# Last row of the third filter tap by TensorE, w1T loaded in three pieces, last blocks of P shared anew

## The chip, the cores and the metric

The kernel runs on one core of a Trainium2 chip. The time is that of the device in microseconds; the kernel before takes 394.8 us (median of three runs, 394.65 to 394.81).

## The reference, cut to what matters

The input x has 16 images of 32 x 32 pixels and 128 channels, in float32. A depthwise 3x3 convolution gives three values a channel (w_perc), a matrix w_up1 takes these 384 to 256 hidden values, then comes an exact GELU, w_up2 back to 128, and the sum with x is h. On h lies a 3x3 windowed attention with w_qkv, and its result is added.

```python
perceived = conv(x, w_perc, groups=C, padding='SAME') + b_perc      # 3C channels
hid = gelu(einsum('bphw,dp->bdhw', perceived, w_up1) + b_up1)       # 2C
h = x + einsum('bdhw,cd->bchw', hid, w_up2) + b_up2
qkv = h @ w_qkv.T + b_qkv
scores = [ (q * shifted(k, dy, dx)).sum(-1) / sqrt(C) for 9 places ]
out = h + sum(softmax(scores)[i] * shifted(v, dy, dx))
```

The depthwise filter and w_up1 are both linear, so the kernel joins them into one 3x3 convolution from 128 to 256 channels.

## The kernel before, in words

**Weights.** For each horizontal tap i (0, 1, 2) and row dy (0, 1, 2) the joined weight is the sum over m of wg[:, m, dy, i] times w1T[:, m, :], where w1T holds w_up1 (128 partitions, three groups m of 256) and wg the filters times -1/6 (L946). Tap 0 and tap 2 are built by ScalarE (m = 0, first_products, L746) and VectorE (m = 1 and 2, L1012), row by row; tap 1 by TensorE (middle_tap, L451) out of nine diagonal matrices that ScalarE makes from the identity (L767). VectorE and ScalarE combine the three taps into six sets of Winograd weights (weff, L1021 to L1041), each split into a high part (whi, L775) and a low part (wlo, L993, L999), as products are taken in fp32r three times over (high x high, high x low, low x high).

**Images.** An image lies as four planes of columns (xp). VectorE forms ab (L960, L962) and four parts of t (transform, L970), GpSimd differences of planes (fc, ge, L1381 to L1385) and two more parts of t (L1389, L1390). ScalarE rounds t to thi (L715), VectorE (GpSimd for image 0) forms tlo (L977). TensorE's products (L484) go in units: an image has two halves of the hidden channels with six units each, and a unit has nine products of up to 256 columns. The sums are taken back by VectorE: combine (ps_sb and ru_sb, L1057, L1058), combine_y (L1067 to L1073) and finish_y (L1081). Then ScalarE's GELU (L731), its rounding (high_hid, L741), the low part on GpSimd (low_hid, L1404), the products up (L539), the sum h (sum_h, L1238), its high and low parts (L816, L987), q, v and scores on TensorE (L575 to L592), the maxima (L1111) and exponentials (L807), the normalising of p on GpSimd (L1411), and its transposition into ptc (turn_p, L1145). Blocks of ptc are moved into pt by DMA (L414, 12 an image); for the last two images these moves are copies, by ScalarE (place, L796), VectorE (L1160) and GpSimd (L1474). The products with v (values, L609) come two images later.

**Order.** It is written by hand for every engine, on each a list of its own in body(n, ...), with images 0 to 3 apart, a loop of ten images, and the last two apart; `last` holds what follows. An engine's instructions start in this order, and semaphores tie the engines together. All large loads are issued by SyncE's queue in program order, w1T first, x_planes of image 0 next; the filters (L708) and the identity (L709) go over ScalarE's queue. All stores are issued by SyncE, the last seven in store_late (L399, L404).

**TensorE's start.** It waits for w1T, issues five fillers (keep_busy, ten passes, as a float32 product takes two), the middle tap (18 passes), small products for the biases and for wq.wk, three more fillers into m_ps (L471, after which VectorE may write there), and then the first products of image 0.

Of the kernel before, what the change touches and what calls it, by code (L numbers as in the profile page):

```python
# [14 lines left out]
P = 128  # L15
# [68 lines left out]
def build(nc, x_planes, x_rows, w_perc, b_perc, w1_c, b_up1, w2_c, b_up2, wqk_c, wv_c, b_qkv, ident_bf_c,  # L84
          mask_c, zero_c, out):
    with ExitStack() as ctx:
# [104 lines left out]
        diag = y_flat[:, 0:9 * P].rearrange("p (m d c) -> p m d c", m=3, d=3)  # L191
        end0 = by_row(ptc[:, :, :].rearrange("p t k -> p (t k)"))
# [5 lines left out]
        first_in = sem("first_in")  # L198
# [16 lines left out]
        tap1_done = sem("tap1_done")  # L215
        first_done = sem("first_done")
# [47 lines left out]
        hlo_done = sem("hlo_done")  # L264
        h_hi_done = sem("h_hi_done")
# [94 lines left out]
        def _(sp):  # L360
# [10 lines left out]
            sp.dma_start(w1T[:, :, :].rearrange("p m d -> p (m d)"), w1_c).then_inc(first_in, 16)  # L371
# [23 lines left out]
            def store_late():  # L395

                for i, (n, g) in enumerate(LATE):
                    sp.wait_ge(o_done, (B - 3) * 2 + i + 1)
                    sp.dma_start(out[n][:, g * CH:(g + 1) * CH],  # L399
                                 o_of(n)[:, g * CH:(g + 1) * CH]).then_inc(stored[g], 16)  # L400
# [35 lines left out]
        def _(pe):  # L436
# [7 lines left out]
            def middle_tap():  # L444

                pe.wait_ge(first_in, 16)
                keep_busy(5)
                for dy in range(3):
                    pe.wait_ge(diag_done, 3 * dy + 3)
                    for m in range(3):  # L450
                        last = pe.matmul(acc[1][:, dy, :], diag[:, m, dy, :], w1T[:, m, :], start=(m == 0),  # L451
                                         stop=(m == 2))
# [82 lines left out]
            def up(n):  # L535
# [20 lines left out]
                pe.wait_ge(hlo_done, n * 2)  # L556
# [57 lines left out]
            def last_attention():  # L614
# [40 lines left out]
                for g in range(2):  # L655
                    pe.wait_ge(pt_done, 12 + 6 * g)
                    pe.wait_ge(pt_dve_done, 12 + 3 * g)
                    if g:
                        pe.wait_ge(pt_pool_done, 3)
# [47 lines left out]
        def _(act):  # L707
# [15 lines left out]
            def gelu(n, half):  # L723
# [4 lines left out]
                if from_image(n, 1):  # L728
# [14 lines left out]
            def first_products(i):  # L743

                for dy in range(3):
# [14 lines left out]
            act.wait_ge(first_in, 16)  # L760
            act.wait_ge(filters_done, 1)
            for i in TAPS:
                first_products(i)
            act.wait_ge(ident_in, 16)
            for dy in range(3):
# [72 lines left out]
            def last():  # L838
# [10 lines left out]
                for g in range(2):  # L849
# [4 lines left out]
                    for row in (0, 1):  # L854
                        place(1, row, range(4 * g, 4 * g + 4))

# [86 lines left out]
        def _(dve):  # L943
# [4 lines left out]
            dve.wait_ge(first_in, 16)  # L948
# [40 lines left out]

            def low_weights(j, k):  # L990
# [12 lines left out]
            for k, i in enumerate(TAPS):  # L1003

                for m in (1, 2):
                    for dy in range(3):
                        if m == 1:
                            dve.wait_ge(first_done, dy + 1 if k == 0 else 6)
# [11 lines left out]
            dve.wait_ge(acc_done, 12)  # L1020
# [152 lines left out]
            def last():  # L1173
# [22 lines left out]
                sums(n, 1)  # L1196
# [320 lines left out]
```

## Time and profile before

| | |
|---|---|
| median of 3 runs | 394.8 us |
| profiled execution | 394.93 us |
| its span | 393.1 us |
| TensorE busy | 382.4 us, 97% |
| TensorE's weight loads | 359.6 us, 91% |
| VectorE busy | 340.3 us, 87% |
| ScalarE busy | 256.5 us, 65% |
| GpSimd busy | 180.0 us, 46% |

The time is that of the whole execution, the span runs from the first instruction to the last. Busy shares are averages over the span and over stages that differ: read them by stretches.

### The profile page before, as it was taken

Reading aid. Unit: us, or ns where it says so; the run is one execution under the profiler, and the core shown is the slowest. Engines: PE = TensorE matmul, PEld = TensorE weight load, DVE = VectorE, ACT = ScalarE, POOL = GpSimd, SP = SyncE. Lnnn points to the kernel's source line nnn. Section 1 sums busy time; section 2 is a strip of 40 time slices with the busy share of each in tenths; the row PEclk is TensorE's granted clock in tenths of the full one; section 3 lists DMA queues with packets and bytes.
Section 4 is the critical chain, followed back from the end, with each engine's and each line's share of the span. In section 5 each row is a group of like instructions: output and inputs, shape, how many; then the busy total and the mean of one; then the engine's idle time right before and its main releaser. Section 6 shows DMA issues by size and latency. Waiting matters only on the chain.

```text
span 393.1 us, 10470 instructions
## 1 busy us (share of the span) xinstructions
PE 382.4 (97%) x3664; PEld 359.6 (91%) x3664; DVE 340.3 (87%) x919; ACT 256.5 (65%) x542; POOL 180.0 (46%) x159
## 2 busy tenths in 40 slices
PE   5999999999999999999999999999999999999995
PEld 4999998999989999999999999999999999999874
DVE  4999999999988889888888988888898888887795
ACT  6645478929485774848477484847748484773893
POOL 5784563646445262635525263552526355132111
PEclk9999999999999999999999999999999999999999
DMA  7420301434151513325150332515033231403003
GB/s 226 183 67 3 121 2 25 139 45 170 31 187 20 171 32 65 141 39 173 25 181 14 74 131 39 173 26 175 21 71 132 39 107 26 121 12 85 3 27 135
DMA packets 56313, 33.98 MB, mean 86 GB/s; under 512 B 47200, under 2 KB 48096, under 8 KB 56288
## 3 DMA queue, kind: packets, MB, share of 16 engines
q1 hardware_dynamic: 56000, 33.61, 30.3%
q8 instruction: 15, 0.25, 0.3%
q10 hardware_dynamic: 288, 0.05, 0.1%
q14 instruction: 10, 0.08, 0.1%
HBM read 19.86 MB, written 8.39 MB: 72 GB/s over the span
## 4 chain that ended last, share of the span: by engine, by line
PE 83%; DVE 11%; issue 2%; DMA 1%; ACT 1%; POOL 0%; DVEq 0%; ACTq 0%
PE m_ps L484 45%; PE work L539 10%; PE s_ps L609 9%; PE work L583 7%; PE s_ps L592 6%; PE s_ps L578 2%; PE s_ps L575 2%; PE s_ps L576 2%; DVE t L970 1%; DMA wp<-w_perc 1%; DVE tlo L977 1%; DVE h_around L1238 1%; DVE h_lo L987 1%; DVE s_ps L1012 1%; PE work L562 1%
## 5 line engine op out<-in xcount | busy, mean ns | idle before, releaser
L484 PE MATMUL m_ps<-thi,whi 128*128 128x256 f32 x558 | 158.9, 285 | 0.9 <-DVE ru_sb L1058 0.8
L484 PE MATMUL m_ps<-thi,wlo 128*128 128x256 f32 x558 | 155.5, 279 | 0.0
L484 PE MATMUL m_ps<-tlo,whi 128*128 128x256 f32 x558 | 154.3, 276 | 0.0
L484 PEld LDWEIGHTS m_ps<-thi,whi 128*128 128x128 f32 x558 | 104.8, 188 | 4.3 <-issue 1.0
L484 PEld LDWEIGHTS m_ps<-tlo,whi 128*128 128x128 f32 x558 | 105.6, 189 | 0.6
L484 PEld LDWEIGHTS m_ps<-thi,wlo 128*128 128x128 f32 x558 | 104.9, 188 | 0.0
L1404 POOL TENSOR_TENSOR hid_lo<-hid,hid_hi 128x1024 fp32r<-128x1024 f32 x30 | 72.2, 2406 | 27.9 <-ACT hid_hi L741 21.4
L1381 POOL TENSOR_TENSOR fc<-xp 128x512 f32<-128x512 f32 x16 | 21.3, 1333 | 98.3 <-DVE tlo L977 91.8
L731 ACT ACTIVATE hid<-y,b1eff 128x1024 f32<-128x1024 f32 x31 | 35.7, 1152 | 33.1 <-DVE y L1081 23.1
L715 ACT CAST thi<-t 128x1024 fp32r<-128x1024 f32 (+1 forms) x32 | 25.1, 832 | 48.6 <-DVE t L970 48.5
L807 ACT ACTIVATE p_sb<-p_sb,negmax 128x101 f32<-128x101 f32 x128 | 46.8, 369 | 6.2 <-DVE negmax L1111 6.1
L1411 POOL TENSOR_TENSOR p_sb<-p_sb,rsum 128x384 f32<-128x384 f32 x32 | 27.8, 870 | 42.7 <-DVE rsum L1134 42.7
L609 PE MATMUL s_ps<-pt,v_sb 128*128 128x192 f32 (+2 forms) x260 | 39.0, 305 | 0.0
L609 PEld LDWEIGHTS s_ps<-pt,v_sb 128*128 128x128 f32 x260 | 37.3, 190 | 0.0
L1057 DVE TENSOR_TENSOR ps_sb<-m,m_ps 128x512 f32<-128x512 f32 x32 | 21.6, 676 | 13.9 <-ACT m L721 13.9
L816 ACT CAST h_hi<-h_around 128x512 fp32r<-128x512 f32 x30 | 18.3, 621 | 22.3 <-DVE h_around L1238 22.2
L741 ACT CAST hid_hi<-hid 128x1024 fp32r<-128x1024 f32 x30 | 31.5, 1050 | 0.2
L583 PEld LDWEIGHTS work<-wvT,h_around 128*128 128x128 f32 x240 | 29.1, 192 | 1.2
L977 DVE TENSOR_TENSOR tlo<-t,thi 128x1024 fp32r<-128x1024 f32 (+1 forms) x30 | 28.7, 999 | 1.3 <-ACT thi L715 1.3
L583 PE MATMUL work<-wvT,h_around 128*128 128x129 f32 x240 | 29.2, 275 | 0.0
L1089 DVE TENSOR_TENSOR v_sb<-work,bv 128x384 f32<-128x384 f32 (+1 forms) x45 | 23.0, 512 | 6.3 <-PE work L583 5.2
L823 ACT ACTIVATE q_sb<-s_ps,bq_s 128x512 f32<-128x512 f32 x30 | 20.6, 688 | 11.4 <-PE s_ps L578 11.3
(156 smaller groups left out, 765.6 us busy)
## 6 DMA issues: line engine op xcount, KB each, us to landing
xp<-x_planes SPq DMA_DIRECT2D x16, 640.0 KB, 5.3
xr<-x_rows SPq DMA_DIRECT2D x16, 512.0 KB, 4.1
out<-o_sb SPq DMA_DIRECT2D x28, 256.0 KB, 4.0
pt<-ptc SPq DMA_DIRECT2D x140, 32.0 KB, 1.9
pt<-ptc SPq DMA_DIRECT2D x28, 28.0 KB, 1.9
out<-y SPq DMA_DIRECT2D x3, 256.0 KB, 2.5
w1T<-w SPq DMA_DIRECT2D x1, 384.0 KB, 3.6
out<-y SPq DMA_DIRECT2D x2, 128.0 KB, 2.4
```

What stands on the lines that cost most here:

```text
L484: last = pe.matmul(bank[:, col + first:col + end], a[:, j, dy, half * P:(half + 1) * P], c[:, par, T_PLACE[j], first + by:end + by], start ...
L539: return pe.matmul(up_bank(n, c), w[:, half * C:(half + 1) * C], h[:, half, c * CH:(c + 1) * CH], **kw)
L583: last = pe.matmul(v_bank(n, part)[:, u * VT:(u + 1) * VT], h_of(n - 1, hp)[:, W + i * P:W + (i + 1) * P], wvT[:, :], start=True, stop=True)
L592: last = pe.matmul(s[row * W:(row + 1) * W, u, :], q_sb[:, q:q + W], h_of(n - 1, hp)[:, q:q + NEAR], start=True, stop=True, skip_group_che ...
L609: last = pe.matmul(o_bank(n, g)[:, (first - g * half) * W:(end - g * half) * W], v_of(n - 3, hp)[:, i, :], pt[:, hp, i, (first - above) * ...
L715: nc.scalar.copy(thi[:, par, part, :], t[:, part, :]).then_inc(thi_done, 1)
L731: nc.scalar.activation(hid[:, half, :].rearrange("p (r k s) -> p k r s", k=K4, s=WIN), y[:, half, :, :].rearrange("p k (r s) -> p k r s", ...
L741: nc.scalar.copy(hid_hi[:, half, :], hid[:, half, :]).then_inc(hhi_done, 1)
L807: nc.scalar.activation(p_sb[:, i, 0:KEYS], p_sb[:, i, 0:KEYS], ACT.Exp, bias=negmax[:, i:i + 1], scale=-1.0, accum_out=p_sum[:, i:i + 1]). ...
L977: nc.vector.tensor_tensor(tlo[:, par, part, :], t[:, part, :], thi[:, par, part, :].bitcast(F32), ALU.subtract).then_inc(tlo_done, 1)
L1404: nc.gpsimd.tensor_tensor(hid_lo[:, half, :], hid[:, half, :], hid_hi[:, half, :].bitcast(F32), ALU.subtract).then_inc(hlo_done, 1)
L1411: nc.gpsimd.tensor_tensor(p_sb[:, tiles, 0:NEAR], p_sb[:, tiles, 0:NEAR], rsum[:, tiles].unsqueeze(2).to_broadcast([P, 4, NEAR]), ALU.mult ...
```

## The change

In words: w1T comes by three DMAs, each with a semaphore of its own. ScalarE makes three diagonals (row_diag) for the last row (dy = 2) of tap 2, and TensorE forms this row out of them ahead of the middle tap; ScalarE and VectorE no longer do. The fillers before it are three instead of five, and the middle tap waits for each diagonal instead of for three. In image 0 GpSimd's differences for image 2 wait until the first four parts of y are done. The low part of the second half of hid of image 0 is formed by VectorE (low_hid_first). In image 2 combine(2, 1) stands between the two groups of maxima. Behind the last image the turn of P's second half comes before VectorE's blocks; GpSimd takes row 3 of tiles 0 to 3 instead of 4 to 7, VectorE row 2 of tiles 0 to 3 and rows 2 and 3 of tiles 4 to 7. The stores of image 14 are issued by ScalarE's queue.

```diff
-            sp.dma_start(w1T[:, :, :].rearrange("p m d -> p (m d)"), w1_c).then_inc(first_in, 16)
+            for m in range(3):
+                sp.dma_start(w1T[:, m, :], w1_c[:, m * HID:(m + 1) * HID]).then_inc(w1_in[m], 16)
...
                 for i, (n, g) in enumerate(LATE):
+                    if n == B - 2:
+                        continue
...
-                pe.wait_ge(first_in, 16)
-                keep_busy(5)
+                pe.wait_ge(w1_in[0], 16)
+                keep_busy(3)
+                for m in (1, 2):
+                    pe.wait_ge(w1_in[m], 16)
+                for m in range(3):
+                    pe.wait_ge(row_diag_done, m + 1)
+                    last = pe.matmul(acc[2][:, 2, :], row_diag[:, m, :], w1T[:, m, :], start=(m == 0), stop=(m == 2))
+                last.then_inc(tap2_done, 1)
                 for dy in range(3):
-                    pe.wait_ge(diag_done, 3 * dy + 3)
                     for m in range(3):
+                        pe.wait_ge(diag_done, 3 * dy + m + 1)
...
-                pe.wait_ge(hlo_done, n * 2)
+                if is_image(n, 1):
+                    pe.wait_ge(hlo_dve_done, 1)
+                else:
+                    pe.wait_ge(hlo_done, n * 2)
...
-                    pe.wait_ge(pt_dve_done, 12 + 3 * g)
-                    if g:
-                        pe.wait_ge(pt_pool_done, 3)
+                    pe.wait_ge(pt_dve_done, 9 + 6 * g)
+                    pe.wait_ge(pt_pool_done, 3)
...
-            for i in TAPS:
-                first_products(i)
+            first_products(0)
             act.wait_ge(ident_in, 16)
+            for m in range(3):
+                nc.scalar.activation(row_diag[:, m, :], ident_bf[:, :], ACT.Copy,
+                                     scale=wg[:, m, 2, 2:3]).then_inc(row_diag_done, 1)
+            first_products(2, range(2))
...
+                act.wait_ge(o_done, (B - 1) * 2)
+                for g in range(2):
+                    act.dma_start(out[B - 2][:, g * CH:(g + 1) * CH],
+                                  o_of(B - 2)[:, g * CH:(g + 1) * CH]).then_inc(stored[g], 16)
...
+            def low_hid_first():
+                dve.wait_ge(hhi_done, 2)
+                nc.vector.tensor_tensor(hid_lo[:, 1, :], hid[:, 1, :], hid_hi[:, 1, :].bitcast(F32),
+                                        ALU.subtract).then_inc(hlo_dve_done, 1)
...
-                    for dy in range(3):
+                    dve.wait_ge(w1_in[m], 16)
+                    for dy in range(3 - k):
                         if m == 1:
-                            dve.wait_ge(first_done, dy + 1 if k == 0 else 6)
+                            dve.wait_ge(first_done, dy + 1 if k == 0 else 5)
...
+            dve.wait_ge(tap2_done, 1)
             nc.vector.tensor_tensor(sum02, tap0, acc[2], ALU.add).then_inc(sums_done, 1)
...
                 sums(n, 1)
+                add_h(n, 1, 1)
+                turn_p(n, 1)
                 dve.wait_ge(ptc_done, n * 2 - 1)
                 dve.wait_ge(o_ready, n * 2 - 4)
+                place(1, 2, range(0, 4))
+                dve.wait_ge(ptc_done, n * 2)
                 for row in (2, 3):
-                    place(1, row, range(0, 4))
-                turn_p(n, 1)
-                add_h(n, 1, 1)
-                dve.wait_ge(ptc_done, n * 2)
-                place(1, 2, range(4, 8))
+                    place(1, row, range(4, 8))
...
-                for g in range(2):
-                    add_zero_keys(n, g)
-                    row_max(n, 1 - par, g, g + 1)
+                add_zero_keys(n, 0)
+                row_max(n, 1 - par, 0, 1)
+                if is_image(n, 2):
+                    combine(2, 1)
+                add_zero_keys(n, 1)
+                row_max(n, 1 - par, 1, 2)
...
                     combine_y(1, 0)
+                    low_hid_first()
                     transform_ab(2, 0)
...
                     sums_ab(1)
+                    pool.wait_ge(y_part_done, 4)
                     differences(2, 0)
                     pool.wait_ge(y_part_done, 8)
                     low_hid(0, 0)
                     return
                 if is_image(n, 1):
-                    low_hid(0, 1)
...
-                pool.wait_ge(ptc_done, B * 2)
+                pool.wait_ge(pn_done, B * 2)
+                pool.wait_ge(ptc_done, B * 2 - 1)
                 pool.wait_ge(o_ready, B * 2 - 4)
-                for rows, there, cols, to_rows, to_there, to_cols in p_blocks(3, range(4, 8)):
+                for rows, there, cols, to_rows, to_there, to_cols in p_blocks(3, range(0, 4)):
```

## Rows read from the trace of the kernel before

**Rows 1.** Busy time by stages: stretch, busy us of TensorE, granted clock, DMA, GB/s

```profile
90.00:360.00 270.00, 269.67 (x2673) 1.00 0.32 88
```

**Rows 2.** Chain of waits, first 40 us: start us, us, what

```profile
0.74 3.77 DMA wp<-w_perc
...
10.11 0.79 DVE s_ps L1012 x2
...
13.87 0.96 DVE m_ps L1024
```

**Rows 3.** TensorE's loads by line: ns min/median/max, first to last start

```profile
L442 PEld LDWEIGHTS work<-w1T x10: 285/337/337, 4.4 to 7.8; 128*128 128x128 f32 x10
...
L451 PEld LDWEIGHTS work<-w1T,y x18: 190/190/337, 8.3 to 12.9; 128*128 128x128 f32 x18
```

**Rows 4.** Timeline of TensorE's loads: start us, us, instruction, idle before

```profile
16.78 0.19 PEld L484 LDWEIGHTS m_ps<-thi,whi 128*128 128x128 f32 x1 [0.17 <-issue]
```

**Rows 5.** DMA issues, first 16 us: queue, KB each, median us to landing

```profile
xp<-x_planes SPq DMA_DIRECT2D x3, 640.0 KB, 4.9
...
w1T<-w SPq DMA_DIRECT2D x1, 384.0 KB, 3.6
...
ident_bf<-identity_bf ACTq DMA_DIRECT2D x1, 32.0 KB, 5.1
zeros<-zero_keys SPq DMA_DIRECT2D x1, 20.0 KB, 2.1
wp<-w_perc ACTq DMA_DIRECT2D x1, 13.5 KB, 3.8
```

**Rows 6.** Timeline of ScalarE, 4 to 10 us

```profile
4.82 1.27 ACT L746 ACTIVATE m_ps<-w1T,wg 128x256 f32<-128x256 f32 x3 [1.64 <-DVE wg L946]
...
7.23 2.72 ACT L767 ACTIVATE y<-ident_bf,wg 128x128 f32<-128x128 bf16 x9
```

**Rows 7.** Timeline of TensorE's loads, after the first products: idle in brackets

```profile
29.54 0.19 PEld L484 LDWEIGHTS m_ps<-thi,whi 128*128 128x128 f32 x1 [0.21 <-issue]
...
34.39 0.19 PEld L484 LDWEIGHTS m_ps<-thi,whi 128*128 128x128 f32 x1 [0.62 <-issue]
...
73.79 0.19 PEld L484 LDWEIGHTS m_ps<-thi,whi 128*128 128x128 f32 x1 [0.58 <-DVE ru_sb L1058]
```

**Rows 8.** Timeline of VectorE and GpSimd, 28 to 75 us

```profile
28.01 2.56 DVE L977 TENSOR_TENSOR tlo<-t,thi 128x1024 fp32r<-128x1024 f32 x2
...
38.65 2.64 DVE L1071 SCALAR_TENSOR_TENSOR y<-ru_sb 128x256 f32<-128x256 f32 x1
...
67.43 1.81 DVE L977 TENSOR_TENSOR tlo<-t,thi 128x1024 fp32r<-128x1024 f32 x2
...
72.46 0.68 DVE L1057 TENSOR_TENSOR ps_sb<-m,m_ps 128x512 f32<-128x512 f32 x1
...
38.61 2.41 POOL L1404 TENSOR_TENSOR hid_lo<-hid,hid_hi 128x1024 fp32r<-128x1024 f32 x1 [0.50 <-ACT hid_hi L741]
...
72.01 2.38 POOL L1404 TENSOR_TENSOR hid_lo<-hid,hid_hi 128x1024 fp32r<-128x1024 f32 x1
```

**Rows 9.** Timelines behind the last image, by engine

```profile
382.82 2.00 DVE L1160 COPY pt<-ptc 32x128 f32<-32x128 f32 x6
384.85 0.58 DVE L1145 STREAM_TRANSPOSE ptc<-p_sb 128x384 f32<-128x384 f32 x1
...
386.81 1.23 DVE L1214 TENSOR_TENSOR y<-m_ps,h_around 128x1024 f32<-128x1024 f32 x1
...
382.87 0.85 POOL L1411 TENSOR_TENSOR p_sb<-p_sb,rsum 128x384 f32<-128x384 f32 x1 [0.75 <-DVE rsum L1134]
...
385.46 1.90 ACT L796 COPY pt<-ptc 32x128 f32<-32x128 f32 x6 [0.82 <-DVE ptc L1145]
...
387.42 1.68 PE L609 MATMUL m_ps<-pt,v_last 128*128 128x32 f32 x10 [0.88 <-ACT pt L796]
...
389.91 0.95 SPq L404 DMA_DIRECT2D out<-y  x2
```

More of the change, by code:

```diff
@@ L191, in build @@
         diag = y_flat[:, 0:9 * P].rearrange("p (m d c) -> p m d c", m=3, d=3)
+        row_diag = y_flat[:, 9 * P:12 * P].rearrange("p (m c) -> p m c", m=3)
         end0 = by_row(ptc[:, :, :].rearrange("p t k -> p (t k)"))
@@ L195, in build @@
         TAPS = (0, 2)
-        first_in = sem("first_in")
+        w1_in = [sem(f"w1_in{m}") for m in range(3)]
         filters_in = sem("filters_in")
@@ L215, in build @@
         tap1_done = sem("tap1_done")
+        tap2_done = sem("tap2_done")
+        row_diag_done = sem("row_diag_done")
         first_done = sem("first_done")
@@ L264, in build @@
         hlo_done = sem("hlo_done")
+        hlo_dve_done = sem("hlo_dve_done")
         h_hi_done = sem("h_hi_done")
@@ L727, in gelu @@
                     act.wait_ge(b1_done, 1)
-                if from_image(n, 1):
+                if is_image(n, 1) and half:
+                    act.wait_ge(hlo_dve_done, 1)
+                elif from_image(n, 1):
                     act.wait_ge(hlo_done, n * 2 + (half - 1))
@@ L741, in high_hid, with first_products @@
                 nc.scalar.copy(hid_hi[:, half, :], hid[:, half, :]).then_inc(hhi_done, 1)
-            def first_products(i):
-                for dy in range(3):
+            def first_products(i, rows=range(3)):
+                for dy in rows:
                     nc.scalar.activation(acc[i][:, dy, :], w1T[:, 0, :], ACT.Copy,
@@ L759, in _ @@
             nc.scalar.activation(primer[:, :], h_around[:, 0, 0:1], ACT.Gelu).then_inc(primed, 1)
-            act.wait_ge(first_in, 16)
+            act.wait_ge(w1_in[0], 16)
             act.wait_ge(filters_done, 1)
-            for i in TAPS:
-                first_products(i)
+            first_products(0)
             act.wait_ge(ident_in, 16)
+            for m in range(3):
+                nc.scalar.activation(row_diag[:, m, :], ident_bf[:, :], ACT.Copy,
+                                     scale=wg[:, m, 2, 2:3]).then_inc(row_diag_done, 1)
+            first_products(2, range(2))
             for dy in range(3):
@@ L947, in _ @@
             dve.wait_ge(filters_done, 1)
-            dve.wait_ge(first_in, 16)
             def rows(a):
@@ L1005, in _ @@
                 for m in (1, 2):
-                    for dy in range(3):
+                    dve.wait_ge(w1_in[m], 16)
+                    for dy in range(3 - k):
                         if m == 1:
-                            dve.wait_ge(first_done, dy + 1 if k == 0 else 6)
+                            dve.wait_ge(first_done, dy + 1 if k == 0 else 5)
                         else:
@@ L1019, in _ @@
             nc.vector.tensor_copy(bq_wide[:, :], bqk[:, 0:1].to_broadcast([P, P])).then_inc(bq_wide_done, 1)
-            dve.wait_ge(acc_done, 12)
+            dve.wait_ge(acc_done, 10)
+            dve.wait_ge(tap2_done, 1)
             nc.vector.tensor_tensor(sum02, tap0, acc[2], ALU.add).then_inc(sums_done, 1)
@@ L1290, in body @@
                     softmax_front(2, 0)
-                    combine(2, 1)
                     sums(2, 0)
@@ L1404, in low_hid @@
                 nc.gpsimd.tensor_tensor(hid_lo[:, half, :], hid[:, half, :], hid_hi[:, half, :].bitcast(F32),
-                                        ALU.subtract).then_inc(hlo_done, 1)
+                                        ALU.subtract).then_inc(hlo_done, 2 if is_image(n, 0) else 1)
             def normalise(n, g):
```

## The prediction

> **What bounds the kernel now.** I read the table of busy time by stages first [rows 1]: from 90 to 360 us TensorE works 269.67 of 270 us at the full clock (1.00), so there every instruction moved off TensorE, or made faster elsewhere, is worth nothing. What an edit can win lies before the first product of the Winograd weights, in the holes of the first four images, and behind the last image, where TensorE stands 0.88 us for one wait alone [rows 9]. The change touches these three places alone. The profiled execution took 394.93 us for a span of 393.1 us (1.83 us lie around it), 0.13 us over the median of 394.8; the sum is made against 394.93.
>
> The chain of waits [rows 2] gives the start: filters' landing, then VectorE's products, with two of them (0.79 us) behind the two halves of the image's ab, then the sum of weights at 13.87 that waits for the middle tap. The loads of TensorE [rows 3, 4] show the other half: fillers from 4.4, middle tap from 8.3 without a pause, and the first product at 16.78 after an idle of only 0.17 us. So TensorE itself is the second bound of the start: VectorE alone could be made 3 us faster, and all but 0.17 us would be lost unless TensorE's own row of work also starts earlier.
>
> **The start, DMAs.** The filters (13.5 KB) land 3.8 us after their issue, about when w1T (384 KB, 3.6 us) does, while the zeros (20 KB) later take 2.1 us [rows 5]. With w1T in three pieces the filters have at best 2.1 us and at worst the 3.8 us of now. I take 2.7 us, a third of the difference, since only a third of w1T is ahead: they land at 3.4 instead of 4.5, VectorE and ScalarE start 1.1 us earlier. The identity (5.1 us now, from an issue at 1.18) lies likewise between 3.3 and 6.3; I take 4.7. Each piece of w1T lies between 2.1 and 3.6 us; the first is taken at 3.1 us from the span's start, the third, issued 0.9 us later, at about 4. Every later load of SyncE's queue is issued 0.9 us later, x_planes among them (4.9 us in the median [rows 5], issued at 1.2 before). It must queue behind w1T either way, so I cost it at nothing; if it keeps its whole 4.9 us it lands at 7.0, GpSimd's three differences (2.7 us) end at 9.7, and VectorE's transforms, due at about 9.0, lose 0.7 us.
> The trace does not say why so small a load takes as long as w1T. The Trainium skill, page "DMA: Bandwidth & Descriptors", section "Queues, rings and completion order", says an engine that has work on two rings takes whole packets from each in turn; by that rule the filters wait for one packet of w1T, a third as large afterwards, which is the case taken here. Were the 3.8 us their own, the start would be the first rival below.
>
> **The start, engines.** ScalarE: three products take 1.27 us [rows 6], from about 3.7 to 5.0; three diagonals of the last row at 0.30 us each (nine took 2.72 us, same rows) end at 5.9; two products of tap two end at 6.7. VectorE's six products of tap zero, 0.39 us each (half of 0.79 [rows 2]), end at 6.7 as well, so its wait for the fifth first product costs nothing, and 1.3 us if the identity comes at 6.3. It has two products fewer: 0.79 us. Together 1.9 us, less 0.4 us that I allow since its ab now falls beside GpSimd's differences: the sum of weights could start 1.5 us earlier.
> TensorE: 10 filler passes and then 18 of the middle tap; its loads took 0.337 us up to about 10.1 us and 0.190 us after [rows 3]: the pace of 1.2 GHz, then of 2.4 GHz, the rise coming 5.8 us into unbroken work. Now 6 filler passes (0.39 us each) from 3.1 to 5.5, 6 passes of the last row (0.42 us each) from 5.5, when its first diagonal is there (5.4), to 8.0. If the rise comes as long after the start as before, at 8.9, two of the 18 are slow and 16 take 0.215 us: 4.3 us, end 12.3 against 13.1. Eight tenths, and the 0.17 us of idle: the first product starts 1.0 us earlier. With the rise at 7 it is 1.5 (VectorE's bound), at 10 it is 0.2. What follows the middle tap on TensorE (3.5 us of small products) is unchanged. GpSimd's low halves of t follow ScalarE's high halves, about 1.7 us earlier, so not late. **Term one: 1.0 us.**
>
> **Images 0 to 3.** TensorE's loads are broken at 29.54, 34.39 and 73.79, by 0.21, 0.62 and 0.58 us [rows 7]. The first ends with tlo of image 1, the second with ru_sb of image 0's second half. VectorE reaches both late because two of its instructions took 2.56 us beside GpSimd's differences and take 1.81 us without [rows 8]. With GpSimd's differences held back behind the four y parts, and VectorE 0.5 us further ahead of TensorE than now, it is 0.7 us early at the second hole: both close. The differences then lie beside additions that read PSUM; such a one at 72.46 takes 0.68 us although GpSimd works from 72.01 for 2.38 us [rows 8]. The second half of hid_lo moves to VectorE: it costs 1.1 us there (two thirds of 1.81 us), but takes away the 2.64 us product that sat through GpSimd's 2.41 us instruction [rows 8], and is worth about 0.4 us by its like (half of 0.79 us, [rows 2]). VectorE gains about 1 us, and the last third of up(1) has its operand at about 38.8 while TensorE comes to it at 39.9. The third hole waits for the second half of the combination that starts at 72.46 [rows 8], which comes 1.3 us earlier, in front of the second group of maxima: it closes; four exponentials on ScalarE start 0.4 us later, under TensorE's work. The stops before h_lo (0.6 us twice, near 64) hang on up(2) and stay. **Term two: 1.4 us.**
>
> **The tail.** VectorE places six blocks (2.00 us) between its two turns of P; the second starts at 384.85 although GpSimd's normalising ended at 383.72 [rows 9]. With one addition of 512 columns out of PSUM (0.68 us, as in [rows 8]) in between instead, it starts at 383.75, 1.1 us earlier. ScalarE's last six blocks (1.90 us) are then bound by its earlier six, end 386.6 instead of 387.36. VectorE still has nine blocks at 0.25 us, held 0.35 us by GpSimd's three: to 386.95. The last ten products start at about 387.0 instead of 387.42, TensorE's idle of 0.88 us before them shrinking by half. VectorE's double addition (1.15) and the next (0.6) end at 388.75, as the last products do. SyncE's last two stores are issued from 389.91 for 0.95 us, the second at about 390.4, behind three others that kept the queue busy; two of those now go over ScalarE's queue. With the operands of the last store at 389.5 and 0.2 us of queue, it is issued at 389.7. Bounds: 0.4 (TensorE's gain alone) and 1.0. **Term three: 0.7 us.**
>
> **Sum:** 1.0 + 1.4 + 0.7 = 3.1 us, 391.8 against 394.93, 391.7 beside the median.
>
> **Rivals.**
> A: the DMAs land as late as before. VectorE waits for the identity, starting tap two 0.3 us late with two products less: 0.5 us won. TensorE's last row then goes from 6.75 to 9.3, the middle tap 9.3 to 13.65, 0.5 us later than now, less 0.17: the start loses 0.35 us. With 1.4 and 0.7: 393.0. For it: 5.1 us for the identity.
> B: a new wait takes the place of the closed holes: VectorE stands for ScalarE's second cast before its hid_lo, up(1) waits, and h_lo comes late. Price up to 1 us: 392.7. Against it 1.1 us of slack.
> C, the other side: in the pause that A leaves between the three fillers (end 5.5) and the last row (6.75), the rise of the clock is postponed. Each us of delay makes the passes in it twice as long and costs 0.5 us. The gains of terms two and three, 2.1 us, less the 0.35, are used up at a rise about 3.5 us later than now, 13.7; at 16 the first product comes 3.25 us late and the kernel takes 396.1. Only unbroken work is seen before the rise here, so the trace cannot exclude it.
> The Trainium skill, page "TensorE: Matmul & The Clock Gate", section "Part 1: The HAM clock gate", says the array is throttled by default and activity releases it: the rule that speaks against cutting fillers. Its own words let the moment vary from run to run; by it, C needs a pause such as A's. This trace agrees in so far as the slow loads stand first.
>
> **Chances.** Forecast 0.60, A 0.15, B 0.12, C 0.05, and 0.08 for more than forecast (DMAs at their lower ends, clock at 7: 1.5 + 1.4 + 1.0 gives 391.0; the stops near 64 gone as well, 390.0). The range is 390.2 to 393.3. A measurement here tells 0.2%, 0.8 us, from no change. Faster 0.91; same 0.05 (0.01 of C, and 0.04 of A together with B or a lost tail); slower 0.04 (the rest of C).
>
> **What would show it.** First filler near 3.1 and wg near 3.4; last row's passes ahead of the middle tap without a pause; first product near 15.8; no idle before the loads of image 1 and ru_sb; hid_lo on VectorE under 1.3 us; the last turn of P near 381.4; two stores on ScalarE's queue. Wrong: wg still at 4.5, loads of 0.337 us beyond 10, or idle before L539 or L578 that was not there.

## The result

The changed kernel takes 395.31 us (median of 22 runs, 394.59 to 397.70) beside 394.80 us for the kernel before (22 runs, 394.62 to 395.02). The ratio is 1.0021, with a 95% interval of 1.0012 to 1.0029: slower by a fifth of a per cent, where 391.7 us and a range of 390.2 to 393.3 were forecast. The runs also spread over 3.1 us where those of the kernel before spread over 0.4.

**Profile after.** The profiled execution took 397.53 us for a span of 394.5 us; it was the second slowest of the 22, so it shows more than the median run has (see the clock below). The chain of waits of its first 30 us (start us, us, what) answers to [rows 2]:

```profile
1.66 0.43 SPq L376
...
2.13 6.08 DMA xp<-x_planes
...
8.29 1.56 POOL fc L1416
9.85 0.82 POOL ge L1419
10.67 0.72 POOL ge L1420
...
12.27 1.61 DVE t L993 x3
...
14.99 0.96 DVE m_ps L1056
```

Before, the chain began with the filters and went through VectorE's products; now it is the load of the image's planes, and behind it GpSimd's differences, which the chain before did not hold. GpSimd's first difference is the first use of the planes; before, its timeline had it 2.13 us earlier:

```profile
6.16 1.32 POOL L1381 TENSOR_TENSOR fc<-xp 128x512 f32<-128x512 f32 x1 [2.48 <-DMA xp<-x_planes]
```

What the change was to bring earlier did come earlier, but for one thing: the third piece of w1T landed at 5.0 us (the first two at 2.9 and 3.5), later than the whole of w1T before, which TensorE could use from 4.38. The DMA issues of the first 16 us (KB each, median us to landing), against [rows 5],

```profile
w1T<-w SPq DMA_DIRECT2D x3, 128.0 KB, 2.3
...
ident_bf<-identity_bf ACTq DMA_DIRECT2D x1, 32.0 KB, 2.4
...
wp<-w_perc ACTq DMA_DIRECT2D x1, 13.5 KB, 2.4
```

and TensorE's loads by line (ns min/median/max, first to last start), against [rows 3]: the middle tap starts 0.4 us earlier and ends 0.9 us earlier.

```profile
L449 PEld LDWEIGHTS work<-w1T x6: 288/338/338, 2.9 to 4.7; 128*128 128x128 f32 x6
...
L464 PEld LDWEIGHTS work<-w1T,y x18: 190/190/332, 7.8 to 12.0; 128*128 128x128 f32 x18
```

But the first product now comes at 17.89 instead of 16.78 [rows 4], behind 2.17 us without a load. The timeline of TensorE's loads (start us, us, instruction, idle before):

```profile
17.89 0.19 PEld L497 LDWEIGHTS m_ps<-thi,whi 128*128 128x128 f32 x1 [2.17 <-issue]
```

And in this execution TensorE was given half its clock for 3.4 us right after. The busy time by stretches (PE, PEld, DVE, ACT, POOL, granted clock, DMA share, GB/s) and one load in it, 0.33 us long as those of 1.2 GHz were at the start:

```profile
16.00:19.00 3.00, 1.20 (x10) 1.11 (x10) 2.99 (x5) 2.30 (x8) 3.00 (x3) 1.00 0.02 7
19.00:22.50 3.50, 3.50 (x19) 3.50 (x19) 3.49 (x5) 1.82 (x3) 3.50 (x4) 0.51 0.02 5
22.50:26.00 3.50, 3.50 (x32) 3.50 (x32) 3.47 (x7) 1.51 (x3) 2.80 (x4) 1.00 0.00 0
```
```profile
20.48 0.33 PEld L497 LDWEIGHTS s_ps<-thi,wlo 128*128 128x128 f32 x1
```

The idle places of [rows 7] are gone, and the two stops before h_lo near 64 us are still there (0.44 and 0.61 us, as before). Two new ones stand further on, at 52.34 and 88.89, of 0.49 and 0.37 us:

```profile
52.34 0.19 PEld L497 LDWEIGHTS m_ps<-thi,whi 128*128 128x128 f32 x1 [0.49 <-issue]
...
88.89 0.19 PEld L594 LDWEIGHTS s_ps<-h_lo,wqk_hi 128*128 128x128 f32 x1 [0.37 <-DVE h_lo L1010]
```

### The profile page after: what moved, and what is told of

Read it like the earlier page. It is cut to its first block, busy times and chain, and to the rows that moved or that the text cites. A ratio compares the mean times of both kernels' runs of the same rounds, so it can differ in the third digit from the quotient of the medians.

```text
span 394.5 us, 10482 instructions
## 1 busy us (share of the span) xinstructions
PE 384.4 (97%) x3666; PEld 361.0 (92%) x3666; DVE 339.6 (86%) x918; ACT 257.4 (65%) x544; POOL 175.6 (45%) x158
## 4 chain that ended last, share of the span: by engine, by line
PE 90%; DVE 5%; DMA 2%; POOL 1%; issue 1%; SPq 0%; DVEq 0%; POOLq 0%
PE m_ps L497 48%; PE work L552 10%; PE s_ps L625 9%; PE work L599 7%; PE s_ps L608 6%; PE s_ps L594 2%; PE s_ps L591 2%; PE s_ps L592 2%; DMA xp<-x_planes 2%; PE s_ps L497 1%; PE work L497 1%; DVE h_around L1270 1%; DVE h_lo L1010 1%; POOL p_sb L1448 1%; PE work L578 1%
## 5 line engine op out<-in xcount | busy, mean ns | idle before, releaser
L1441 POOL TENSOR_TENSOR hid_lo<-hid,hid_hi 128x1024 fp32r<-128x1024 f32 x29 | 69.7, 2404 | 25.1 <-ACT hid_hi L758 20.9
L1000 DVE TENSOR_TENSOR tlo<-t,thi 128x1024 fp32r<-128x1024 f32 (+1 forms) x30 | 27.9, 972 | 1.3 <-ACT thi L730 1.3
L843 ACT ACTIVATE q_sb<-s_ps,bq_s 128x512 f32<-128x512 f32 x30 | 20.6, 688 | 11.4 <-PE s_ps L594 11.4
```

The source lines that it names most:

```text
L1000: nc.vector.tensor_tensor(tlo[:, par, part, :], t[:, part, :], thi[:, par, part, :].bitcast(F32), ALU.subtract).then_inc(tlo_done, 1)
L1441: nc.gpsimd.tensor_tensor(hid_lo[:, half, :], hid[:, half, :], hid_hi[:, half, :].bitcast(F32), ALU.subtract).then_inc(hlo_done, 2 if is_i ...
```

## Experiments

Each kernel was run against the kernel before on the same chip; times are medians.

**1. w1T in one DMA again.** The changed kernel, with

```diff
-            for m in range(3):
-                sp.dma_start(w1T[:, m, :], w1_c[:, m * HID:(m + 1) * HID]).then_inc(w1_in[m], 16)
+            sp.dma_start(w1T[:, :, :].rearrange("p m d -> p (m d)"), w1_c).then_inc(w1_in[0], 16)
```

> The changed kernel with w1T in one DMA again. Theory T1 (the split put the load of x_planes 0.93 us later in SyncE's queue and spread its landing over the 16 engines, so that it landed at 8.2 us instead of 6.1, and the whole start waited for it): x_planes lands at 6.1 to 6.4 us, the filters again at about 4.5, the first product of image 0 at 16.3 to 17.2, no fall of the clock behind it, time 392.5 to 393.8. Rival T2 (the extra row on TensorE and the identity set the start, not the DMAs): first product stays near 17.9, time 394.6 or more.

Measured: 393.86 us (12 runs, 393.30 to 396.08) beside 394.79; ratio 0.9986, interval 0.9974 to 0.9998. Undoing this one edit makes the changed kernel 1.45 us faster, and faster than the kernel before. GpSimd's first difference, which waits for the planes, and the first product, in the timelines of GpSimd and of TensorE's loads:

```profile
5.81 1.32 POOL L1415 TENSOR_TENSOR fc<-xp 128x512 f32<-128x512 f32 x1 [2.13 <-DMA xp<-x_planes]
```
```profile
16.39 0.19 PEld L496 LDWEIGHTS m_ps<-thi,whi 128*128 128x128 f32 x1 [0.94 <-issue]
```

T1 holds in kind, with numbers somewhat off: the planes were used from 5.81 us (6.1 to 6.4 expected), the filters from 4.16 (4.5), and the median is 0.06 us above its range. The granted clock does not fall behind the first product. T2 falls.

**2. The split alone.** The kernel before, with its load of w1T replaced by the three, and waits for the pieces in the places of those for w1T:

```diff
-            sp.dma_start(w1T[:, :, :].rearrange("p m d -> p (m d)"), w1_c).then_inc(first_in, 16)
+            for m in range(3):
+                sp.dma_start(w1T[:, m, :], w1_c[:, m * HID:(m + 1) * HID]).then_inc(w1_in[m], 16)
```

> The kernel before with nothing changed but w1T in three DMAs, as in the changed kernel. T1: x_planes lands at about 8 us instead of 6.1, GpSimd's differences end at about 10.9 or later, VectorE's transforms start at about 11.2 instead of 10.9 at the least, the first product comes 0.8 to 1.3 us later, time 395.5 to 397 with more spread between runs than the kernel before. Rival T2: filters land earlier and x_planes does not matter, time 394.8 or less.

Measured: 396.28 us (8 runs, 395.10 to 396.90) beside 394.79, +1.49 us; ratio 1.0037, interval 1.0026 to 1.0047. The two timelines:

```profile
8.50 1.56 POOL L1384 TENSOR_TENSOR fc<-xp 128x512 f32<-128x512 f32 x1 [4.82 <-DMA xp<-x_planes]
```
```profile
18.10 0.19 PEld L487 LDWEIGHTS m_ps<-thi,whi 128*128 128x128 f32 x1 [2.42 <-issue]
```

The split costs the same 1.5 us in the median whether put into one kernel or taken from the other, so nothing else of the change is needed for the loss. The medians of the spans agree less well: 1.5 us here, 1.1 us between experiment 1 and the changed kernel; the rest of that lies outside the span, on which see "The sum".

**3. The planes over ScalarE's queue.** The changed kernel; load_planes(0, 0) leaves SyncE's list and stands behind the identity on ScalarE's.

```diff
+            act.dma_start(xp[:, 0, :, :, :].rearrange("p k r w -> p (k r w)"), x_planes[0]).then_inc(x_loaded[0], 16)
```

> The changed kernel with the load of x_planes of image 0 issued by ScalarE's queue behind the identity, 0.45 us earlier than on SyncE's queue. T1, if the place in the issue order counts: lands at 7.0 to 7.7, first product 0.5 to 1.2 us earlier than in the changed kernel, time 392.5 to 394. T1, if it is the share of the engines' time among many small loads: no earlier than 8, same time as the changed kernel or slower. T2: no difference in time.

Measured: 395.47 us (12 runs, 394.44 to 397.00) beside 394.79. GpSimd's first difference starts at 8.50 us: an earlier issue on another queue lands no earlier. The time is that of the second reading of T1, and of T2 as well. But this start is bound elsewhere: the third piece of w1T took 6.54 us to land, TensorE stood 3.08 us for it before its last row, and the first product came at 18.67 with no pause before it. From the chain of waits:

```profile
1.66 6.54 DMA w1T<-w
```

So the run shows that the other queue does not bring the planes earlier; that the queue makes no difference it does not show.

**4. More fillers.** The changed kernel, so that TensorE has work while it waits:

```diff
-                for _ in range(3):
+                for _ in range(7):
                     last = pe.matmul(m_ps[:, 2, S:CH], w1T[:, 0, 0:P], w1T[:, 0, 0:S], start=True, stop=True)
```

> The changed kernel with seven instead of three fillers behind the small products, so that TensorE is not idle from 15.5 to 17.9 us. Theory T3 (the spread of 394.6 to 397.7 and some 1.5 us of the profiled run come from the fall of the granted clock to a half from 19.1 to 22.5 us, behind that idle time): no fall after the first product, runs within 0.4 us of each other, median 394.0 to 394.8. Rival (the spread comes from when the loads land): the spread of more than 2 us stays.

Measured: 395.24 us (12 runs, 394.18 to 396.45) beside 394.79. The profiled execution shows no half clock behind the first product, but one execution cannot show that it never comes; the runs still spread over 2.3 us, and the median stands where the changed kernel's does. With 1.5 us, the price of the fall as worked out below, taken off the five longest spans of the changed kernel, its median would be 0.16 us lower, an estimate: the fall costs single executions and little of the median. T3 is wrong about the spread as a whole: 5 of these 12 runs are 3.0 us or more over their span. With the loads of the changed kernel GpSimd's first difference stood earlier here, at 7.84 us:

```profile
7.84 1.32 POOL L1416 TENSOR_TENSOR fc<-xp 128x512 f32<-128x512 f32 x1 [4.16 <-DMA xp<-x_planes]
```

**5. Stores on SyncE.** As 1, and the two stores of image 14 issued by SyncE again:

```diff
-                    if n == B - 2:
-                        continue
...
-                act.wait_ge(o_done, (B - 1) * 2)
-                for g in range(2):
-                    act.dma_start(out[B - 2][:, g * CH:(g + 1) * CH],
-                                  o_of(B - 2)[:, g * CH:(g + 1) * CH]).then_inc(stored[g], 16)
```

> The changed kernel with w1T in one DMA, and the two stores of image 14 issued by SyncE again. Theory T4 (the runs of the changed kernel lie up to 3.3 us over their span against 1.83 us before, because the last stores go over ScalarE's queue too): runs 1.8 to 2.1 us over the span, spread below 0.5 us, median 393.2 to 393.9. Rival (the spread comes from the start, where fillers and loads stand otherwise): the spread of the one-DMA kernel, 393.3 to 396.1, stays; median 0.2 to 0.7 us above 393.86, as SyncE's queue is full at the end again.

Measured: 393.73 us (12 runs, 393.25 to 395.52) beside 394.83. The spread is 2.3 us where 0.5 was expected, and its profiled execution (394.76 us) lies 3.3 us over its span, so the second queue is not needed for such a run: T4 falls. Nor is the median higher than that of 1, so the second queue brings nothing: the last stores landed at 391.01 us with it and at 391.02 without, in executions whose last part of VectorE ran 0.06 us apart.

**6. Images alone.** The kernel before with the edits of images 0 to 3:

```diff
                     sums_ab(1)
+                    pool.wait_ge(y_part_done, 4)
                     differences(2, 0)
...
+                    low_hid_first()
...
+                if is_image(n, 2):
+                    combine(2, 1)
```

> The kernel before with only the edits of images 0 to 3 (GpSimd's differences held back, hid_lo of image 0 on VectorE, combine(2, 1) between the maxima). By term two of the prediction: the idle before the loads at 29.5, 34.4 and 73.8 us goes, 393.2 to 393.6. Rival (the holes come back as others, as one of 0.5 us at 52 us and two of 0.4 and 0.1 us at 88 us did in the changed kernel): 394.0 to 394.5.

Measured: 394.05 us (11 runs, 393.37 to 394.40) beside 394.83, 0.78 us less; ratio 0.9981, interval 0.9972 to 0.9990. That is at the lower edge of the rival's range and above the forecast's. The three idle places are gone, and two new ones are there without the rest of the change (TensorE's loads):

```profile
49.15 0.19 PEld L485 LDWEIGHTS m_ps<-thi,whi 128*128 128x128 f32 x1 [0.48 <-issue]
```
```profile
85.74 0.19 PEld L582 LDWEIGHTS s_ps<-h_lo,wqk_hi 128*128 128x128 f32 x1 [0.36 <-DVE h_lo L993]
```

**7. Tail alone.** The kernel before with the edits behind the last image (both stores over ScalarE's queue among them):

```diff
                 sums(n, 1)
+                add_h(n, 1, 1)
+                turn_p(n, 1)
...
-                for rows, there, cols, to_rows, to_there, to_cols in p_blocks(3, range(4, 8)):
+                for rows, there, cols, to_rows, to_there, to_cols in p_blocks(3, range(0, 4)):
```

> The kernel before with only the edits behind the last image. By term three: 394.0 to 394.4, spread as before. Rival (VectorE's nine blocks and additions now set the end, and ScalarE's queue for the stores costs outside the span): span 0.4 us shorter but the median at 394.6 to 395.5, with runs up to 3.3 us over the span.

Measured: 394.40 us (12 runs, 393.94 to 395.51) beside 394.83, 0.43 us less; ratio 0.9995, interval 0.9986 to 1.0004. Nine runs lie at 394.56 or below, three at 395.40 to 395.51. The time alone hides what happened: the median of the spans is 0.65 us shorter than before, and the three late runs are 3.1 to 3.3 us over their spans, where no run of the kernel before is more than 1.93 over its own. The rival had that part right. TensorE's first product of the Winograd weights in this execution, whose start is that of the kernel before:

```profile
16.45 0.19 PEld L486 LDWEIGHTS m_ps<-thi,whi 128*128 128x128 f32 x1 [1.24 <-issue]
```

**8. w1T in two.** The changed kernel with one DMA for the first third and one for the rest:

```diff
+            sp.dma_start(w1T[:, 0, :], w1_c[:, 0:HID]).then_inc(w1_in[0], 16)
+            sp.dma_start(w1T[:, 1:3, :].rearrange("p m d -> p (m d)"), w1_c[:, HID:3 * HID]).then_inc(w1_in[1], 16)
```

> The changed kernel with w1T in two DMAs, the first third and the rest. T1a (the loads' engines starve while descriptors of many small DMAs are made, so the number of DMAs ahead of x_planes counts): x_planes lands between 6.5 and 7.5 us, first product 0.5 to 1.0 us earlier than in the changed kernel (17.9), time 393.8 to 394.8. T1b (a split of w1T into rows of 1 or 2 KB is enough): lands at 8 as with three, time 395.3.

Measured: 394.09 us (8 runs, 393.02 to 395.39) beside 394.83; ratio 0.9979, interval 0.9965 to 0.9993. GpSimd's first difference starts at 7.09 us, 5.4 us after the planes' issue at 1.66; first product at 16.64. Between one piece (393.86) and three (395.31), nearer to one: T1a.

**9. The start alone, w1T in one DMA.** The kernel before with row_diag, the three fillers and the row of tap 2 on TensorE:

```diff
+                for m in range(3):
+                    pe.wait_ge(row_diag_done, m + 1)
+                    last = pe.matmul(acc[2][:, 2, :], row_diag[:, m, :], w1T[:, m, :], start=(m == 0), stop=(m == 2))
```

> The kernel before with the start of the changed one (last row of tap two by TensorE, three fillers, three diagonals), but w1T in one DMA; images and tail as before. T5 (the row on TensorE by itself wins nothing: VectorE loses two products but waits for the identity, and small products follow the middle tap as before): first product within 0.2 us of the kernel before's, time 394.6 to 395.1. Rival by the prediction's term one: first product 0.3 us or more earlier, time 394.4 or less.

Measured: 394.88 us (11 runs, 394.45 to 395.21) beside 394.83; ratio 1.0001, interval 0.9992 to 1.0010. TensorE's loads run on without a pause up to the first product:

```profile
15.81 1.17 PEld L480 LDWEIGHTS m_ps<-w1T 128*128 128x128 f32 x6
17.01 0.19 PEld L493 LDWEIGHTS m_ps<-thi,whi 128*128 128x128 f32 x1
```

T5 holds in time: the row on TensorE wins nothing. Its reason is in the chain of waits and in ScalarE's timeline: the identity took 5.29 us to land, and ScalarE stood for it before it could make the diagonals of the row and, behind them, the first products of tap two that VectorE needs.

```profile
1.19 5.29 DMA ident_bf<-identity_bf
```
```profile
6.50 0.98 ACT L774 ACTIVATE y<-ident_bf,wg 128x128 f32<-128x128 bf16 x3 [0.88 <-DMA ident_bf<-identity_bf]
```

TensorE without a pause is not the reason: in experiments 1 and 5, with the same start, it stood 0.94 and 1.02 us before the first product, which came at 16.39 and 16.41. That is no earlier than without the row (16.23 to 16.78 in before and experiments 6, 7 and 10), and their chains begin with the identity too.

**10. Images and tail, no start.** The kernel before with the edits of 6 and 7.

> The kernel before with the edits of images 0 to 3 and of the tail, nothing of the start. If the parts add: -0.78 and -0.43 us from the runs of each alone, 393.6, and the fastest of all kernels here. Rival: the holes closed and the tail lean on the same idle time, 393.9 to 394.1.

Measured: 393.56 us (8 runs, 393.45 to 394.85) beside 394.83, 1.27 us less; ratio 0.9974, interval 0.9964 to 0.9985. The parts add, and no kernel here has a lower median. Its five lowest runs lie within 0.12 us, the other three at 394.47 to 394.85: two of them over 3 us above their spans, the third, which was profiled, with a span of 393.1 us where the others have 391.3 to 391.8. Lines on the DMA issues behind 385 us in it, and in experiment 1 behind 384 us:

```profile
out<-y SPq DMA_DIRECT2D x1, 256.0 KB, 4.7
out<-y SPq DMA_DIRECT2D x2, 128.0 KB, 3.7
```
```profile
out<-y SPq DMA_DIRECT2D x1, 256.0 KB, 2.9
out<-y SPq DMA_DIRECT2D x2, 128.0 KB, 3.0
```

**11. The planes first.** The changed kernel with load_planes(0, 0) ahead of the three pieces.

> The changed kernel with x_planes of image 0 issued ahead of the three pieces of w1T. If the engines starve behind the split pieces whatever comes next: x_planes lands at about 5.2 us or earlier, the pieces of w1T after it at 5 to 6. If the starving belongs to a moment of the start (3.2 to 4.4 us) and not to the pieces, x_planes itself is hit and lands after 6. First filler at 5 or later, so the time is 395 or more either way.

Measured: one execution, 396.42 us. GpSimd starts at 4.66 us: the planes are not hit, and a starving tied to a moment of the start falls. The pieces land at 5.0 to 5.8 us, TensorE starts at 5.07, and the first product comes at 18.25 with no pause before it: the planes early and w1T late is no gain.

```profile
4.66 1.32 POOL L1416 TENSOR_TENSOR fc<-xp 128x512 f32<-128x512 f32 x1 [0.97 <-DMA xp<-x_planes]
```

**12. Two small loads ahead.** The kernel before, w1T whole, with

```diff
+            sp.dma_start(bp[:, :], b_perc.rearrange("(c m) -> c m", m=3)).then_inc(biases_in, 16)
+            sp.dma_start(b2[:, :], b_up2.rearrange("(p a) -> p a", a=1)).then_inc(biases_in, 16)
             load_planes(0, 0)
...
-            sp.dma_start(bp[:, :], b_perc.rearrange("(c m) -> c m", m=3)).then_inc(biases_in, 16)
...
-            sp.dma_start(b2[:, :], b_up2.rearrange("(p a) -> p a", a=1)).then_inc(biases_in, 16)
```

> The kernel before, w1T in one DMA, with the two small loads of b_perc and b_up2 ahead of x_planes, which is thus issued 0.93 us later, as in the changed kernel. T1c (the later issue alone makes it late): x_planes lands at 7 to 8 us and the time is 395.3 or more. T1d (the pieces of w1T do it: with their short rows the engines run dry before the next descriptors are there): lands at 6.0 to 6.6, with DMA throughput above 300 GB/s from 3.2 to 4.8 us, time 394.8 to 395.1.

Measured: 395.28 us (11 runs, 395.02 to 396.41) beside 394.83; ratio 1.0015, interval 1.0006 to 1.0024. GpSimd starts at 7.07 us, 4.9 us after the planes' issue at 2.13; before, it was 5.0 us after the issue at 1.20:

```profile
7.07 1.32 POOL L1381 TENSOR_TENSOR fc<-xp 128x512 f32<-128x512 f32 x1 [3.39 <-DMA xp<-x_planes]
```

Both readings are half right: 0.9 us of the delay of the planes is the issue alone (T1c), and a further 0.8 to 1.4 us, from 7.07 to the 7.84, 8.29 and 8.50 of experiment 4, the changed kernel and experiment 2, come only with the pieces. One execution of each was profiled, and single executions scatter: with the loads in the order of before the first difference started at 5.77 to 6.70 us in seven of them. The medians say the same: +0.45 us here, +1.49 with the pieces.
The throughput over the first 16 us shows where. Each number is a slice of 0.4 us, and the ninth to the twelfth are those from 3.2 to 4.8 us; before, after, and this kernel:

```profile
GB/s 0 0 0 0 108 179 285 239 358 424 424 390 344 350 325 230 74 95 243 179 51 346 358 384 318 300 428 358 410 379 374 425 392 353 384 256 179 64 0 0
```
```profile
GB/s 0 0 0 0 56 249 300 254 156 74 169 225 320 346 310 343 361 258 141 182 235 176 159 305 385 384 351 341 394 410 369 399 358 346 358 333 346 307 166 90
```
```profile
GB/s 0 0 0 0 84 146 326 382 160 212 218 346 384 335 292 361 275 190 261 323 57 205 384 358 279 292 430 399 440 399 422 443 402 445 410 256 90 0 0 0
```

Before, the engines go from w1T straight to the planes at 358 to 424 GB/s. In the other two they have little to move after 3.2 us: 74 to 225 GB/s in the four slices after it in the changed kernel, 160 to 218 in the first three here, and then 346.

## Why the prediction was wrong

**What bounds the kernel.** Right for the middle: from 90 to 360 us TensorE works the same 269.67 us in both, and the differences inside the span lie where the text put them. (That an instruction moved off TensorE would be worth nothing there goes too far: it would be worth its own time. The change moves none there.)
For the start it rested on one execution. TensorE's idle time of 0.17 us before the first product made it the second bound; in experiments 6, 7 and 10, with the same start, it was 1.24 to 1.27 us. The sum of weights at 13.87 did not wait for the middle tap either: VectorE had no idle time before it. In the executions profiled of before, after and experiments 1, 2, 4 to 8, 10 and 12, the first product starts 2.90 us after VectorE's sum of weights, however long TensorE had stood (2.99 us in experiment 9). So VectorE's chain was the bound, and what delays it, as late planes do, is paid.

**The start, DMAs: the step that failed.** "It must queue behind w1T either way, so I cost it at nothing." The terms I took for the small loads were too cautious (filters 2.4 us against 2.7 taken, identity 2.4 against 3.5), and the term at nothing was the whole loss of the start: the split alone costs 1.49 us (experiment 2). The bound beside it, landing at 7.0 for 0.7 us, was too small as well: the planes were used from 8.29. Two things were missed. First, planes issued 0.93 us later do not queue behind w1T: in experiment 12 the engines have done with w1T and stand with little to move, so the later issue is paid in full (7.07 us, 0.45 us of time). Second, the pieces cost a further 0.8 to 1.4 us, which the trace of before could not show; behind three short pieces issued in a row the engines move 74 to 225 GB/s up to 4.8 us in the changed kernel, and 64 to 190 in experiment 2. I bounded the landing from one side by issue plus the duration from a row, and the row was one of a single large DMA ahead; the bound above was open.
From there the first product follows by the chain: GpSimd's differences end at 11.4 instead of 8.8 us, VectorE's four transforms behind them, the sum of weights at 14.99 instead of 13.87, first product 1.11 us later instead of 1.0 us earlier.

**The start, engines.** ScalarE and VectorE kept the times of the text nearly to the tenth: products from 3.81, three diagonals, two products up to 6.8, VectorE's products of tap two from 6.86 (6.7 forecast). The faster pace of TensorE's loads, 0.19 us, came by 8.98 us (forecast for its first case: 8.9), 6.05 us into its work, and the middle tap ended at 12.2 (12.3). That this agreed is luck: in experiment 4, with the same start, the faster pace came 3.0 us into the work, in experiment 6, with the start of before, 3.4 us, where the execution that the forecast was read from had 5.9. (In this stretch the profile gives the granted clock as 1.00 throughout; both levels, 1.2 and 2.4 GHz, are read here from the loads alone.)
TensorE's own row of work ended at 15.7 us, so it would have allowed a first product 1 us earlier; whether VectorE would have kept up with the planes on time, no run shows. With w1T whole, the filters are used from 4.06 and the identity lands at 6.5, and the gain is 0 (experiment 9): the split is what brings the small loads early and what makes the planes late. For the identity the two are one thing in part: in experiment 12, with w1T whole and the planes issued 0.93 us later, it took 3.2 us instead of 5.1.

**Images 0 to 3.** 1.4 us forecast, 0.78 us measured (experiment 6). The three holes closed as the text said; hid_lo on VectorE took 1.22 us (1.1). The step that failed in size is that a closed hole is a gain: TensorE then comes 1 us earlier to tlo of image 2, which waits for ScalarE's thi, and to h_lo of image 3, and stands there for 0.48 and 0.36 us. Rival B in kind, at other places than I had named and without ending the gain.

**The tail.** 0.7 us forecast, 0.43 us of time measured (experiment 7), at its lower bound of 0.4, though the interval of its ratio includes no change. Inside the span it was right: 0.65 us. In the profile of after the second turn of P starts 1.6 us after the first instead of 2.7 [rows 9], as forecast, and ScalarE's twelve blocks run through:

```profile
383.94 0.58 DVE L1177 STREAM_TRANSPOSE ptc<-p_sb 128x384 f32<-128x384 f32 x1
...
385.52 0.58 DVE L1177 STREAM_TRANSPOSE ptc<-p_sb 128x384 f32<-128x384 f32 x1 [0.36 <-POOL p_sb L1448]
386.13 2.23 DVE L1192 COPY pt<-ptc 32x128 f32<-32x128 f32 x9
388.39 1.23 DVE L1246 TENSOR_TENSOR y<-m_ps,h_around 128x1024 f32<-128x1024 f32 x1
```

The part of it that I gave to the second queue for stores is nothing (experiment 5). What failed is a term that the sum did not have: it carried the 1.83 us around the span over unchanged, and these edits lengthen them (below).

**Rivals and the clock.** A (loads as late as before) did not come about in the changed kernel; its mechanism, the late identity, is what experiments 1, 5 and 9 show with w1T whole. C named the clock, with the right kind of place, work after a pause, and the wrong pause: not between fillers and last row (0.4 us in the trace), but the 2.2 us of waiting before the first product, followed 1.2 us later by 3.4 us at half the clock. In the profiled execution, TensorE's first load of the scores of image 0 stands at 50.54 us, 1.71 us later than before, in experiment 1 at 47.52; counted from the first product that makes 32.65 against 31.13 us, so the half clock took 1.5 us. Such a pause does not always bring it: in the execution of experiment 2 TensorE stood 2.42 us at the same place, and the granted clock was 1.00 up to 30 us. The Trainium skill ("TensorE: Matmul & The Clock Gate", section "Part 1: The HAM clock gate") gives an idle engine the lower clock; the trace of the changed kernel agrees, with a delay, and that of experiment 2 does not show it. In the 22 runs, five have spans of 394.3 us or more, with a mean granted clock of 0.990 to 0.996; the others have spans of 391.8 to 393.1. That the clock fell in just these five is likely and not shown, as three of the others have 0.996 as well.

**The sum.** Inside the span the parts add up, by medians of the spans: images -0.8 us (experiment 6), tail -0.65 (experiment 7), and the start with the split +1.35 (the changed kernel beside experiment 10) make -0.1; measured is a span 0.2 us shorter than before, 392.8 against 393.0. The time is 0.5 us longer all the same, as what lies outside the span grew by 0.65 us in the median. Against the forecast the start is 2.35 us off, the images 0.6, what lies outside the span 0.65, and the tail next to nothing.

| kernel | edits of the tail | median of the spans, us | median outside, us | runs over 2.5 us outside |
|---|---|---|---|---|
| before | no | 393.0 | 1.82 | 0 of 88 |
| split alone (2) | no | 394.45 | 1.80 | 0 of 8 |
| images alone (6) | no | 392.2 | 1.82 | 0 of 11 |
| tail alone (7) | yes | 392.35 | 1.97 | 3 of 12 |
| images and tail (10) | yes | 391.45 | 2.05 | 2 of 8 |
| changed, w1T whole (1) | yes | 391.7 | 2.06 | 2 of 12 |
| changed | yes | 392.8 | 2.47 | 11 of 22 |

All 129 runs of kernels without the edits of the tail (before and experiments 2, 6, 9 and 12) lie 1.74 to 1.93 us over their spans. Of the 98 with them (the changed kernel and experiments 1, 3, 4, 5, 7, 8 and 10) 29 lie 2.6 to 3.6 us over. So the edits of the tail bring this, and by themselves (experiment 7); the second queue for the stores is not needed for it (experiment 5, 1 of 12). Which of the others does it, and how, is open. It was more frequent with w1T in pieces (21 of 54 runs) than whole (8 of 44), which no run explains.
Apart from this, a store can lengthen the span itself: in experiment 10 the last one took 4.7 us to land instead of 2.9.

## What to carry to other kernels

A load that is split so that its first part comes early moves every later load of its queue: ask which of these the start will then wait for, and cost it as issue time plus its full duration, not as hidden behind the load that was split. Two small loads put ahead of the planes cost 0.45 us (experiment 12); but the planes put ahead of w1T brought no gain either (experiment 11), so the order has to serve both chains. An idle time or a moment of the clock read from one execution is one draw: the same start gave 0.17 and 1.24 us of idle time. And what lies outside the span is part of the time: compare it too, run by run. Before an idle place of the bounding engine is counted as won, look for the next instruction of the same engine whose operand has less slack than that.

## What the runs showed of the hardware

Three short DMAs ahead of a 640 KB one made it land 0.8 to 1.4 us later than its issue alone explains: it was used at 7.07 us with w1T whole and two small loads ahead, at 7.84, 8.29 and 8.50 us with w1T in three, and at 8.50 us too when another queue carried it. Why the engines have so little to move in these is open.
A load of 13.5 KB on another queue took 3.2 to 3.8 us beside one DMA of 384 KB (eight executions) and 2.3 to 2.4 us beside three of 128 KB (four). That fits the rule of the Trainium skill that the prediction weighed ("DMA: Bandwidth & Descriptors", section "Queues, rings and completion order"), by which an engine with work on two rings takes packets from them in turn.
In the changed kernel the lower clock came 1.2 us after TensorE had resumed work from a pause of 2.17 us, not during the pause; in experiment 2, after a pause of 2.42 us, the granted clock stayed at 1.00.
The pace of TensorE's loads rose 3.0 to 6.2 us after its first load in twelve executions, in kernels whose starts are the same by 3.4 to 5.9 us.
